# A transformer layer on eight cores: softmax without its shift, column sums tile by tile, and W2 steps moved

## What is computed

```python
q = (q_input @ Wq.T + bq).reshape(B, T, N_HEADS, HEAD_DIM).transpose(0, 2, 1, 3)
k = q_input @ Wk.T + bk
v = q_input @ Wv.T + bv
mask = pos[None, :] < pos[:, None]
scores = jnp.einsum('bhtd,bsd->bhts', q, k) * scale
scores = jnp.where(mask[None, None, :, :], scores, NEG_BIG)
attn = jax.nn.softmax(scores, axis=-1)
out = jnp.einsum('bhts,bsd->bhtd', attn, v)
...
out = out @ Wo.T + bo
...
hidden = jax.nn.silu(up_gate) * up_lin
hidden = fwht(hidden)
out = jnp.einsum('bsh,dh->bsd', hidden, W2)
...
x = _layernorm(x + attention(x))
x = _layernorm(x + ffn(x))
```

## Time and profile before

| | us |
|---|---|
| three runs, median (lowest to highest) | 5087.89 (5059.03 to 5241.28) |
| the profiled execution | 5066.88 |
| its span, slowest core (core 7) | 5065.2 |
| spans of the eight cores | 5005.0 to 5065.2 |
| PE busy | 3018.4 |
| DVE busy | 958.6 |
| ACT busy | 823.9 |

### The profile page before, as it was taken

How to read it: one execution, slowest core, us unless ns; L and a number is a source line. 1 busy time by engine, 2 the same in 40 slices (tenths; PEclk the granted TensorE clock), 3 DMA queues, 4 the chain that set the end, 5 groups by cost and what they waited for, 6 DMA issues and landing times.

```text
span 5065.2 us, 30224 instructions; the slowest of 8 cores (5005.0 to 5065.2 us)
## 1 busy us (share of the span) xinstructions
PE 3018.4 (60%) x9689; PEld 970.7 (19%) x9689; DVE 958.6 (19%) x1623; ACT 823.9 (16%) x1392; POOL 149.9 (3%) x280
## 2 busy tenths in 40 slices
PE   4576334444444444444336668888888888783763
PEld 1222000000000000000002223333333333231321
DVE  1122433232222222222111420000000000003003
ACT  1111122222222222222110221111111100000000
POOL 1000000000000000000000000000000000000000
PEclk8777555555555555555557778888888777776997
DMA  5311200000000000000222121111111111332332
GB/s 174 101 67 61 76 25 13 13 13 13 13 13 13 13 13 13 0 13 25 76 78 85 53 75 54 54 50 57 52 54 55 50 46 58 106 98 97 110 113 96
DMA packets 96479, 276.83 MB, mean 55 GB/s; under 512 B 11716, under 2 KB 11844, under 8 KB 91976
## 3 DMA queue, kind: packets, MB, share of 16 engines
q0 software_dynamic: 34512, 139.48, 9.2%
q1 hardware_dynamic: 61816, 135.43, 8.2%
HBM read 224.54 MB, written 50.33 MB: 54 GB/s over the span
## 4 chain that ended last, share of the span: by engine, by line
PE 49%; DMA 15%; DVE 14%; ACT 13%; issue 7%; DVEq 0%; ACTq 0%; SPq 0%; POOL 0%; POOLq 0%
PE pb L180 49%; ACT GA L454 8%; DMA W2P<-GA 7%; DMA GA<-W2P 6%; DVE RR L489 2%; DVE GA L235 2%; ACT GA L231 2%; DVE pb L451 2%; DVE GA L682 2%; DVE GA L472 1%; DVE GA L475 1%; DMA GA<-X1S 1%; ACT GA L693 1%; DMA GA<-XBT 1%; ACT GA L679 1%
## 5 line engine op out<-in xcount | busy, mean ns | idle before, releaser
L180 PE MATMUL pb<-GA 128*128 128x512 bf16 x8576 | 2521.0, 446 | 910.0 <-ACT GA L454 649.3
L180 PEld LDWEIGHTS pb<-GA 128*128 128x128 bf16 x8576 | 857.5, 106 | 2545.0 <-issue 2017.0
L180 PE MATMUL pb<-GA,CB 64*64 64x512 bf16 (+2 forms) x824 | 436.2, 554 | 797.7 <-DVE GA L235 246.1
L454 ACT ACTIVATE GA<-pb,MNEG 128x512 bf16<-128x512 f32 x576 | 395.8, 687 | 975.5 <-PE pb L180 679.3
L682 DVE TENSOR_TENSOR GA<-GA,pb 128x512 bf16<-128x512 f32 x128 | 88.0, 688 | 1220.7 <-PE pb L180 1097.2
L180 PEld LDWEIGHTS pb<-GA,CB 64*64 64x64 bf16 (+2 forms) x824 | 87.9, 109 | 1143.3 <-issue 1142.1
L235 DVE CAST GA<-pb 64x512 bf16<-64x512 f32 x256 | 164.0, 678 | 557.0 <-DMA W2P<-GA 535.4
L231 ACT CAST GA<-pb 64x512 bf16<-64x512 f32 x256 | 135.7, 578 | 472.7 <-DMA W2P<-GA 416.2
L693 ACT ACTIVATE GA<-pb 128x512 bf16<-128x512 f32 x128 | 76.5, 597 | 614.2 <-PE pb L180 614.2
L679 ACT ACTIVATE GA<-pb 128x512 f32<-128x512 f32 x128 | 76.0, 594 | 523.8 <-PE pb L180 523.8
L747 DVE TENSOR_TENSOR GA<-pb,GA 128x512 f32<-128x512 f32 x32 | 20.6, 686 | 697.6 <-DMA GA<-X1S 367.5
(11 more groups left out here) (80 smaller groups left out, 570.2 us busy)
## 6 DMA issues: line engine op xcount, KB each, us to landing
GA<-W2P SPq DMA_DIRECT2D x256, 256.0 KB, 2.5
GA<-W2T POOLq DMA_DIRECT2D x128, 256.0 KB, 3.7
W2P<-GA SPq DMA_DIRECT2D x128, 256.0 KB, 4.0
GA<-W1S POOLq DMA_DIRECT2D x64, 512.0 KB, 3.8
GA<-W3S POOLq DMA_DIRECT2D x64, 512.0 KB, 3.7
GA<-XBT POOLq DMA_DIRECT2D x8, 2048.0 KB, 10.9
GA<-WQS POOLq DMA_DIRECT2D x4, 2048.0 KB, 9.5
GA<-XOWN SPq DMA_DIRECT2D x1, 8192.0 KB, 27.7
```

Of the source, the lines that this page charges most:

```text
L180: return e.matmul(out, lhsT, rhs, start=start, stop=stop, skip_group_check=True)
L454: texp = em.op("s", lambda e, qp=qp, slot=slot, g=g: e.activation(pbuf[slot], qp[:], AF.Exp, bias=MNEG[:, g:g + 1], scale=SC), waits=_mx(d ...
```

## The change

Three things are changed.

- The norm work of K and of Q and the chain that makes `MNEG` are removed, with the tiles `MNEG`, `MT` and `ksq`. The exp in attention has no bias: softmax is computed without a shift.
- The column sums are taken tile by tile: behind each AV matmul stands a matmul of the same exponentials against `ONEC`, and the three additions on VectorE are gone. `pbuf` has four slots in use, each free when its sum matmul is done.
- The W2 steps stand elsewhere: two behind every group of attention (64) and one behind each of the 32 groups of the output projection. The output projection uses banks 0 to 5 in turn and leaves 6 and 7 to the steps; the transposes of the layer norm use banks 4 and 5.

The diff, cut to its core:

```diff
-        tk2 = em.op("v", lambda e: e.memset(MT[0:1, 0:1], 0.0))
-        ksq_rd = None
-        for blk in range(8):
-            tq = em.op("v", lambda e, blk=blk: e.tensor_mul(
...
@@ Q projection, behind each eviction @@
-                    tq = em.op("v", lambda e, h=h, th=th: e.tensor_mul(
-                        ksq, qT[:, h * 1024 + th * 512:h * 1024 + th * 512 + 512],
...
-                    tmm = em.op("t", lambda e: MM(e, pb[6][0:1, :], ONEC, ksq, True, True),
-                                waits=_mx(tq, ps_tok[6]))
...
-        tMN = em.op("s", lambda e: e.copy(MNEG[:], pb[7][:, 0:4]), waits=_mx(t8))
...
@@ attention @@
-                            pbuf[slot], qp[:], AF.Exp, bias=MNEG[:, g:g + 1], scale=SC),
-                            waits=_mx(dep, tMN, pbuf_rd[slot]))
+                            pbuf[slot], qp[:], AF.Exp, scale=SC),
+                            waits=_mx(dep, pbuf_rd[slot]))
...
-                    pa = em.op("v", lambda e, exps=exps, sA=sA: e.tensor_add(
-                        pbuf[sA], pbuf[exps[0][1]], pbuf[exps[1][1]]),
...
-                    sum_mm = em.op("t", lambda e, sA=sA, c=c, k=k: MM(
-                        e, pb[4][0:1, :], ONEC, pbuf[sA], c == 0, c == k),
-                        waits=_mx(pc, rs_rd if c == 0 else None, tCB))
+                        rs_mm = em.op("t", lambda e, slot=slot, first=first,
+                                      last_av=last_av: MM(
+                            e, pb[4][0:1, :], ONEC, pbuf[slot], first, last_av),
+                            waits=_mx(rs_rd, tCB) if first else ())
+                        pbuf_rd[slot] = rs_mm
...
-                if g % 2 == 1:
-                    p0_step()
-                    p0_step()
-                    p0_step()
+                p0_step()
+                p0_step()
         tAT = _mx(*attnT_wr)
-        while p0_state["i"] < 128:
-            p0_step()
-        p0_done = _mx(*p0_state["done"])
...
@@ output projection @@
-                po = pb[k]
+                po = pb[k % 6]
...
                 if oc == 3:
                     oproj_done[k] = ta
+                p0_step()
+        while p0_state["i"] < 128:
+            p0_step()
+        p0_done = _mx(*p0_state["done"])
...
-                bank = 6 + c % 2
+                bank = 4 + c % 2
```

More of the change, by code:

```diff
@@ L376, in build_program @@
[L376 to L381, removed]
                 p0_step()
         tQT = _mx(*qT_wr)
-        t1 = em.op("s", lambda e: e.activation(MT[0:1, 32:48], MT[0:1, 16:32], AF.Ln,
-                                               bias=EPSB[0:1, 0:1]),
-                   waits=_mx(tq2m, tEPS))
@@ L388, in build_program @@
[L388 to L410, removed]
-        tMN = em.op("s", lambda e: e.copy(MNEG[:], pb[7][:, 0:4]), waits=_mx(t8))
-        ps_tok[7] = tMN
-        rb2_rd = [t8, None]
+        rb2_rd = [None, None]
         tR = em.op("y", lambda e: e.dma_start(
@@ L424, in build_program @@
         recB_rd = [None, None]
-        pbuf_rd = [None] * 8
+        pbuf_rd = [None] * 4
         attnT_wr = []
@@ L453, in build_program @@
                                 waits=_mx(mm, tMask))
[L454 to L456 removed]
+                        texp = em.op("s", lambda e, qp=qp, slot=slot: e.activation(
+                            pbuf[slot], qp[:], AF.Exp, scale=SC),
+                            waits=_mx(dep, pbuf_rd[slot]))
                         qk_rd[bank] = texp
[L458 removed]
                         first = (c == 0 and q4 == 0)
                         last_av = (c == k and q4 == 3)
[L461 to L462 removed]
+                        em.op("t", lambda e, avp=avp, slot=slot, sig=sig,
+                              first=first, last_av=last_av: MM(
                             e, avp[:], vP[:, sig * 128:sig * 128 + 128], pbuf[slot],
@@ L465, in build_program @@
                             waits=_mx(texp, tVP, av_rd[avbank] if first else None),
-                            inc=(q4 == 3))
-                    sA = 4 + (c % 2)
-                    sB = 6 + (c % 2)
-                    pa = em.op("v", lambda e, exps=exps, sA=sA: e.tensor_add(
-                        pbuf[sA], pbuf[exps[0][1]], pbuf[exps[1][1]]),
[L471 to L479, removed]
-                    sum_mm = em.op("t", lambda e, sA=sA, c=c, k=k: MM(
-                        e, pb[4][0:1, :], ONEC, pbuf[sA], c == 0, c == k),
-                        waits=_mx(pc, rs_rd if c == 0 else None, tCB))
-                    pbuf_rd[sA] = sum_mm
-                    pbuf_rd[sB] = pc
+                            inc=False)
+                        rs_mm = em.op("t", lambda e, slot=slot, first=first,
[3 more added lines that the diff above has]
+                        pbuf_rd[slot] = rs_mm
                 r1 = em.op("v", lambda e: e.tensor_scalar_add(RR[0:1, 0:512], pb[4][0:1, :], 1e-30),
-                           waits=_mx(sum_mm, rr_war[0]))
+                           waits=_mx(rs_mm, rr_war[0]))
                 rr_war[0] = None
@@ L495, in build_program @@
                            waits=_mx(r4, rb2_rd[1]))
-                b1 = em.op("t", lambda e: MM(e, pb[5][:], ONER, RB2[0:1, 0:512], True, False),
-                           waits=_mx(r3, rb_rd))
+                em.op("t", lambda e: MM(e, pb[5][:], ONER, RB2[0:1, 0:512], True, False),
+                      waits=_mx(r3, rb_rd), inc=False)
                 b2 = em.op("t", lambda e: MM(e, pb[5][:], ONER, RB2[0:1, 512:1024], False, True),
                            waits=_mx(r5))
-                rb2_rd = [b1, b2]
+                rb2_rd = [b2, b2]
                 rsl = (k * NG + g) % 2
@@ L508, in build_program @@
                     dst, avp[:], recB[rsl]),
-                    waits=_mx(av_mm, rc, q_last_mm if first_attnT else None))
+                    waits=_mx(rs_mm, rc, q_last_mm if first_attnT else None))
                 first_attnT = False
@@ L513, in build_program @@
                 attnT_wr.append(tv)
-                if g % 2 == 1:
-                    p0_step()
-                    p0_step()
-                    p0_step()
+                p0_step()
+                p0_step()
         tAT = _mx(*attnT_wr)
-        while p0_state["i"] < 128:
-            p0_step()
-        p0_done = _mx(*p0_state["done"])
         wo_rd = [_mx(tAT), _mx(tAT)]
[L524 to L528, removed]
+        obank_rd = {i: _mx(qk_rd[i] if i < 2 else None,
+                           av_rd[i] if i in (2, 3) else None,
+                           rs_rd if i == 4 else None,
+                           rb_rd if i == 5 else None) for i in range(6)}
         oproj_done = [None] * J
@@ L540, in build_program @@
                         h == 0, False),
-                        waits=_mx(tl, opsum_rd[k]) if h == 0 else (), inc=False)
+                        waits=_mx(tl, obank_rd[k % 6]) if h == 0 else (), inc=False)
                 em.op("t", lambda e, po=po, oc=oc: MM(
```

33 lines of the change are left out of this document (5 added, 28 removed).

## The result

The changed kernel takes 4872.7 us (median; lowest 4840.0), a ratio to the kernel before of 0.961 with a 95% interval of [0.956, 0.966]. It is faster by about 4%. The profiled execution is 4872.7 us too, with a span of 4870.9 on core 0; the page of before was that of core 7.

A forecast was written before the change was run, and what follows sets the result against it. TensorE runs its list in order, each seam a wait, so distances between PE starts count. From 5066.9 us: -17 - 89 - 8 + 193 + 70 - 330 + 120 + 3 = -58, so 5009 us; range 4910 to 5095.

The forecast's parts named there:

- the lifted clock in attention: Attention: more matmuls lift its clock to the 2.4 GHz level, -147 us instead of +193, 4669 us in all; chance 4%.
- the slow rival: Both stages interleaved with W2 steps: the clock drops to 1.2 GHz and stays there, 5197 us in all; chance 6%.
- the missing overlap: Each W2 step among the output matmul groups waits a full store besides the group, 5106 us in all; chance 5%.
- exp to AV 0.83: Attention tile: the time from exp to AV, kept at its old 0.83 us within a tile of 2.58 us.
- The row sums: Attention: one sum matmul per tile makes each block of four tiles 1.34 us longer, +193 us over 144 blocks.
- W2 steps in attention: Two steps behind every group cost 10.0 us each, against 15.6 for three behind every second group: +70 us.
- Behind attention: The stretch of W2 steps alone before the output matmuls goes; 5 us are left for the first WOS load: -330 us.
- Output projection: 32 matmul groups, each followed by a W2 step, at 7.4 us, plus 18 for load collisions: 255 us, +120.
- the floor of 6.9: W2 steps among the output matmul groups: the chain, 350.9 us for 51 steps, repeats no faster than 6.9 us.
- Q projection: 16 heads with dense parts of 7.7 us and gaps of 3.1, plus 6 for loads: 176 us against 265, -89.
- the clock stays up: Rival: gaps short enough in both dense stages, no collisions; Q 160, output 221, 50 us less, 4959 us; chance 15%.
- The rule against the row: Sum matmul to next score: the trace's 0.52 us followed over the skill's 427 ns whatever the weights; 0.47 taken after AV.

## Why the prediction was wrong

The structure held. Nothing was seen of the lifted clock in attention, of the slow rival or of the missing overlap, and each stage moved the way it was said to. The sign of the sum was right and its size was not. Two steps failed: the exp was kept at its old time though its bias goes, and the W2 steps were priced too high in their new places and too low in their old ones. A large loss and two large gains stood against each other, and each was mis-sized in the same direction: the norm part measured -176 for -114, the W2 steps -211 (193 by the stages) for -140, the sums +185 for +193.

**The exp in a tile of attention: the step that failed most.** I kept "exp to AV 0.83" and priced only what the change did to PE. The diff takes the bias from the exp, and I put that at nothing. It is 89 ns on each of 576 tiles, 51 us, shown by the run with a tile of zeros; exp to AV is 0.74.

**The row sums: right by luck.** Two more rows of the tile were mis-sized. I took 0.76 from score to exp for every tile. That is what the one tile in four behind a column sum took, because its exp waited for the additions too; the others took 0.73, and a tile now takes 0.70: 32 us less. In the other direction AV to sum is 0.52, my upper bound, and not 0.47: 27 us more. These two nearly cancel, and so the +193 stands close to the 185 measured. With the exp the tile is 2.48 in place of 2.58: 58 of the 86 us by which attention missed.

**W2 steps in attention: a row misread.** I let PE go free behind the pair that starts at 1543.79. A step is four matmuls, two and then two that wait for its first evictions. The row that counts is the one ahead of it:

```profile
1542.25 1.20 PE L180 MATMUL pb<-GA,CB 64*64 64x512 bf16 x2 [3.95 <-DVE GA L235]
```

This pair was the end of the second step and 1543.79 the start of the third. The changed kernel shows the real seam, from the second broadcast matmul to the next score:

```profile
1139.60 0.58 PE L177 MATMUL pb<-RB,CB 1*128 1x512 bf16 x1 [0.72 <-DVE RB L414]
1140.11 1.06 PE L177 MATMUL pb<-GA,CB 64*64 64x512 bf16 x2
1141.61 1.08 PE L177 MATMUL pb<-GA,CB 64*64 64x512 bf16 x2 [0.44 <-ACT GA L228]
1143.03 1.08 PE L177 MATMUL pb<-GA,CB 64*64 64x512 bf16 x2 [0.34 <-ACT GA L228]
1148.65 1.20 PE L177 MATMUL pb<-GA,CB 64*64 64x512 bf16 x2 [4.53 <-DVE GA L232]
1149.78 0.61 PE L177 MATMUL pb<-GA 128*128 128x512 bf16 x1
```

Here 10.2 us, and 9.85 in the median, of which 0.5 would be there without steps: 9.35 in place of 10.0. The first seam was 17.9 us long, with a W2 store that took 11.8 us beside the 8 MB load of `XOWN`. With it the mean over the 31 seams inside attention is 9.6, so they cost 12 us less than I had. The 15 old ones were 16.1 to 17.8 us long, 16.9 in the mean, where I used the one row of 16.1: another 12 us.

**Behind attention.** Right: -336 against -335. The first WOS load is covered by the last two steps but for some 4 us.

**Output projection.** The seam was right, the floor of 6.9 was not. Two windows, each from one group's bias matmuls to the next group's:

```profile
2432.42:2438.57 6.15, 5.39 (x24) 1.94 (x23) 0.69 (x1) 2.12 (x4) 0.52 (x1) 1.00 0.26 72
2438.57:2446.77 8.20, 6.80 (x23) 2.24 (x23) 3.34 (x5) 0.00 (x0) 0.52 (x1) 0.79 0.24 76
```

The first distance is 6.15 us at the full clock. The second is 8.20, with part of the group at the lower clock; most of the 28 that meet no WOS load are one of these two or 6.6. In the drained stretch a step repeated every 6.9 us with the clock at 0.50, and I took this for a floor that the store sets. It is none, as the 6.15 shows; which part of the chain became shorter was not tried by a run. The three groups that meet a WOS load are 13.1, 9.3 and 13.8 us apart; the chain of waits shows the store of one:

```profile
2469.93 9.81 DMA W2P<-GA
```

They last 36.2 us together, and the other 28 distances are 6.85 in the mean: 16 us for the collisions (18 forecast) and 0.55 less per group than the 7.4 forecast.

**Q projection.** The heads' gaps are 2.6 and 3.1 to 3.4 us as worked out, with one beside a WQS load 5.1. The clock is 0.93 instead of 0.75, and a dense part takes 7.35 us in the mean where I had 7.7. This is core 0; on cores 2 and 3 of the same execution the clock of the stage was 0.77 and attention began 26 and 29 us later.

```profile
210.74 7.08 PE L177 MATMUL pb<-GA 128*128 128x512 bf16 x31
217.75 0.62 PE L177 MATMUL pb<-GA,CB 64*64 64x512 bf16 x2
219.15 0.37 PE L177 MATMUL pb<-GA,CB 64*64 64x512 bf16 x1 [0.79 <-DVE GA L232]
...
220.06 7.08 PE L177 MATMUL pb<-GA 128*128 128x512 bf16 x32
```

So the rival "the clock stays up" was largely true in both dense stages of this core, by some 30 us of its 50, though the collisions that it left out did happen.

**The sum and its bounds.** The terms do add up to -58. The bounds don't: with the stated low and high ends they give -148 and +31 (4919 and 5098 us), not -162 and +55, and the low end of the Q projection, with no collisions, is -111 and not -105. None of them holds the 51 us of the exp; with these the low end would be -199, beside the -194 measured.

**The rule against the row.** The Trainium skill ("TensorE: Matmul & The Clock Gate", section "Back-to-back issue gap") gives N/1.2 ns as the gap of matmuls at the low clock, in a formula for a single matmul that has no term for the weights; "whatever the weights" was my reading of it. Where the weights keep their shape the runs are near its 0.427: 0.43 with the four sums together, 0.38 and 0.42 with wide ones. Between shapes they are not: 0.52. Weighing the rule against the row was right.

## What to carry to other kernels

When an edit touches an instruction inside a serial chain, price the instruction again, its operands and its waits too: 0.09 us on 576 serial tiles was a quarter of the whole gain. When several large terms of both signs make the sum, a run with one part at a time (here -176, +185, -211) tells far more than the total. A row stands for the tile it was read from: the 0.76 was one in four. And before moving work about in such a chain, look whether its order can be broken: putting the next score ahead of this AV was worth 3.6 times the whole change (0.925 to 0.785, against 1 to 0.961).

## What I had not expected of the hardware

- An exp of 128x512 out of PSUM takes 687 ns with a [128, 1] bias tile and 598 without, also when the tile holds zeros.
- Behind a 128-wide matmul, one against a single column of weights starts 0.52 us later at the low clock, one against 128 columns of the same ones 0.38 to 0.43.
- The clock of attention stayed at 0.50 in the changed kernel, also inside a block, where three matmuls and a wait of 0.84 repeat. With the next score ahead it was 0.50 in the ends of the groups and the W2 steps and rose to 1.00 inside the long rows of blocks, for 406 of 1164 us; ahead of the rise at 1449.8, PE had run thirteen matmuls from 1443.66 on with one idle stretch of 0.41. With the four sums of a block together it rose for short stretches only, 79 us in all. The busy share of a whole stage doesn't tell these apart (1096 of 2047 us and 623 of 1164 us are the same share), because it averages over both levels. Which feature lifts the clock was not tried.
